# One TensorE stream, another order: the weighted sum between scores 1 and 2, misc work behind score 3

## The chip, the cores and the metric

The kernel runs on one core of a Trainium2 chip. Its time is the device time of one execution in microseconds (us), the median of three runs. TensorE (PE) multiplies matrices, VectorE (DVE) and ScalarE (ACT) work on rows of elements, GpSimd (POOL) does small work and indirect transfers, SyncE (SP) issues most transfers. The engines run their own instruction streams and wait for each other on semaphores.

## The reference, cut to what matters

```
x: (8, 512, 128); 16 heads of 8; 8 experts of 256, top 2
h = layernorm(x) * (1 + ca) + sa
q, k, v = h @ binarized(Wq, Wk, Wv).T + biases        # per head: 512 x 8
att = softmax(q k^T / sqrt(8)); y = att v; x = x + ga * (y @ Wp' + bp)
h = layernorm(x) * (1 + cb) + sb
x = x + gb * (shared_expert(h) + sum over the top 2 experts of weight * expert(h))
```

The attention is computed for 8 batches x 16 heads x 512 queries x 512 keys. That is where the change lies. The experts follow it.

## The kernel before, in words

**Batches and slots.** The attention of a batch is cut into 16 slots (SLOTS). Slot n holds four heads of group n // 4 and 128 keys (n % 4). For each of the four heads hh it makes a score tile of 128 keys x 512 queries (`scores`, `st`), which ScalarE exponentiates into `pt` (`exponentials`), and a weighted sum of all four heads (`products`, `pv`) which adds into one PSUM bank over eight slots. The sum of slot n-1 is issued in slot n. After eight slots ScalarE copies the bank to `y_strips` (`evacuate_y`), and the first sum of the next eight waits for that copy (`y_evacuated`).

**Maxima.** A softmax needs each query's maximum over all keys before its scores are used. Eight slots ahead of their use, TensorE computes the same scores in the other orientation (`max_scores`, a pair of matmuls into one of two `mx` banks, half heads each), and VectorE reduces a pair to the negative maximum (`maxima`, `neg_max`). A slot holds two such pairs, called A and B here; slots 0 to 4 of the first batch hold three. `max_T` turns the maxima of four heads into rows, `split_max` on VectorE splits them, and SyncE stores them as extra rows of the queries' stack, so that a score comes out with its maximum already taken off.

**Banks.** Scores alternate between two banks, so score hh waits until the exponential two before it is done. Maxima alternate between two banks as well, so a pair waits until VectorE has reduced the pair two before it. In the last eight slots of the last batch there are no maxima left; scores 2 and 3 then use the free `mx` banks, and a score waits for the exponential four before it (`wide`).

**Misc work.** Everything else shares a single bank, `misc`: projections and transposes of the batch two ahead, of the one before, router logits, ranks. The use of this bank is a fixed chain: each user waits until the evacuation of the one before it is done (`free(done)` on `misc_free`). `between` issues what belongs to a slot: m1, m2, m3 (`max_T`) in slots 1, 5, 9, y1, yT, out in 2, 3, 4, ln1 in 7, q in 8, h2T in 10, y0 in 11, lg (`router_logits`) in 12, k in 14. Behind the weighted sum stand v (`project_v`) in slot 0, m0 for the next batch in 12 and ranks in 15. VectorE and ScalarE take up the results of misc in the same slot: ScalarE behind its four exponentials, VectorE at the place that the change moves. Their larger pieces are `residual_sum` and `stats2` (slot 4), `split_max` and `layer_norm1` (5), `layer_norm2` (7), `likeliest` (13), `choose` (14), `assign_rows` (15).

**Order.** The order is written out by hand in the `body` functions. On TensorE a slot is: score 0, score 1, pair A, misc, score 2, pair B, score 3, weighted sum of slot n-1.

Of the kernel before, what the change touches and what calls it, by code (L numbers as in the profile page):

```python
# [18 lines left out]
SLOTS = G * TT  # L19
# [28 lines left out]
def adaln_block(nc: bass.Bass, x, Wq, bq, Wk, bk, Wv, bv, Wp, bp, sh_gate, sh_up, sh_down,  # L48
                gate_w, up_w, down_w, router_w, routing_bias, c, wmod, out):
    ctx = ExitStack()  # L50
    with ctx:
# [904 lines left out]
        def _(dve):  # L956
# [163 lines left out]
            def body(b, first, last):  # L1120
                for n in range(SLOTS):
                    fills = fills_at(b, n)
                    maxima(fills[0])
                    if n == 0 and first:
                        for i, w in enumerate("qk"):
                            first_part(dve, B1, i, use(AHEAD, w + "_1"))
# [22 lines left out]
                        add_router_bias(b.plus(-1), use(b, "lg"))  # L1149
                    if n in (13, 14) and not first:  # L1150
                        (likeliest, choose)[n - 13](b.plus(-1))
                    maxima(fills[1])
                    if n == 12 and not last:
                        split_max(b.plus(1), 0, use(b, "m0"))
                    if n == 15 and not first:
# [164 lines left out]
        def _(pe):  # L1320
# [203 lines left out]
            def between(b, n, first, last):  # L1524
# [25 lines left out]
                if n == 14 and b.const < B - 2:  # L1550
                    project(1, use(b, "k"))

            def body(b, first, last):
                for n in range(SLOTS):
                    g, j = n // TT, n % TT
                    fills = fills_at(b, n)
                    if j == 0:
                        pe.wait_ge(m_row_loaded[g % 2], ROW_DMAS * (2 * b.n + g // 2 + 1))
                        if b.const == 0 and g < DIRECT:
                            pe.wait_ge(stack_loaded[0][g], STACK_DMAS)  # L1560
                    scores(b, n, 0)
                    scores(b, n, 1)
                    for f in fills[0]:
                        max_scores(*fill_of(f))
                    between(b, n, first, last)
                    scores(b, n, 2)
                    for f in fills[1][:1]:
                        max_scores(*fill_of(f))
                    scores(b, n, 3)
                    for f in fills[1][1:]:  # L1570
                        max_scores(*fill_of(f))

                    if n > 0:
                        products(b, n - 1)
                    elif not first:
                        products(b.plus(-1), SLOTS - 1)
                    if n == 0 and not last:
                        project_v(use(b, "v"))
                    if n == 12 and not last:
                        max_T(b.plus(1), 0, use(b, "m0"))  # L1580
                    if n == 15 and not first:
                        ranks(b.plus(-1), use(b, "rank"))
# [132 lines left out]
```

## Time and profile before

| | us |
|---|---|
| median of 3 runs | 664.68 |
| lowest, highest | 662.48, 667.34 |
| the profiled execution's span | 683.7 |
| attention in it, first to last exponential | 41.9 to 482.3 |
| a steady batch in it | 55.8 |

The page gives each engine's busy share: TensorE 91%, VectorE 76%, ScalarE 60%, GpSimd 39%. The profiled execution is longer than the plain runs; its rows are used for durations and for the order of things. In a timeline, instructions of one form that follow each other are one row: its start, the time from the first start to the last end, and their count. The end of a matmul is modelled, so the distance of two starts is the better measure of what a matmul costs.

### The profile page before, as it was taken

What the parts mean: (1) busy time and instruction counts of PE and PEld (TensorE: products, weight loads), DVE (VectorE), ACT (ScalarE), POOL (GpSimd) and SP (SyncE); (2) the same over time, 40 slices, a digit from 0 to 9 for tenths busy, and PEclk for the clock granted to TensorE, in tenths of its full rate; (3) what the DMA queues carried; (4) which work ended last, traced back from release to release, by engine and by line L of the source; (5) the groups of instructions that cost most, each with busy time, mean ns of one, the idle gap of its engine ahead of it and who ended that gap; (6) DMA issues with size and microseconds to landing.
All of it is one profiled execution on the core that took longest, in us unless ns stands there. A gap on an engine that the chain in (4) does not pass through costs nothing.

```text
span 683.7 us, 11593 instructions
## 1 busy us (share of the span) xinstructions
PE 624.5 (91%) x3693; PEld 298.9 (44%) x3693; DVE 516.7 (76%) x1104; ACT 411.0 (60%) x846; POOL 264.0 (39%) x309
## 2 busy tenths in 40 slices
PE   4988999999999999999999999999998898888935
PEld 2332333233333333433333333232465888888931
DVE  5659888889988989888898888983368655555617
ACT  2145777777777687777777777778542445444520
POOL 4221022324352461452434233134434366566540
PEclk9669999999999999999999999999999999999987
DMA  3533132222321233223222231115102222222228
GB/s 101 146 56 97 52 101 76 66 82 72 94 86 62 75 97 95 79 78 105 72 70 75 70 98 52 39 40 173 53 0 70 64 74 78 69 78 79 70 68 320
DMA packets 50064, 56.92 MB, mean 83 GB/s; under 512 B 10281, under 2 KB 39243, under 8 KB 50004
## 3 DMA queue, kind: packets, MB, share of 16 engines
q1 hardware_dynamic: 42648, 43.11, 22.4%
q0 software_dynamic: 4320, 8.47, 3.6%
q10 hardware_dynamic: 3036, 4.61, 2.1%
q8 instruction: 30, 0.49, 0.3%
q14 instruction: 30, 0.25, 0.1%
HBM read 38.36 MB, written 17.92 MB: 82 GB/s over the span
## 4 chain that ended last, share of the span: by engine, by line
PE 68%; DVE 13%; ACT 6%; DMA 4%; issue 4%; SPq 2%; POOL 1%; another core or an unknown queue 0%; ACTq 0%; POOLq 0%; DVEq 0%
PE pv L1457 15%; PE st L1446 14%; PE mx L1431 13%; PE st L1646 9%; DVE neg_max L1012 6%; PE mx L1590 3%; ACT pt L803 2%; PE misc L1324 2%; PE misc L1351 2%; PE pv L1655 2%; PE misc L1655 2%; PE st L1600 1%; PE misc L1357 1%; DMA even_qk<-k_parts 1%; DVE ln L969 1%
## 5 line engine op out<-in xcount | busy, mean ns | idle before, releaser
L803 ACT ACTIVATE pt<-st 128x512 f32<-128x512 f32 x496 | 282.2, 598 | 106.0 <-PE st L1446 96.8
L1012 DVE TENSOR_REDUCE neg_max<-mx 128x2 f32<-128x1024 f32 x248 | 294.4, 1215 | 50.5 <-PE mx L1431 47.3
L1457 PE MATMUL pv<-pt,vs 128*32 128x512 f32 x1024 | 136.4, 605 | 0.3 <-ACT pt L803 0.3
L690 POOL DMA_INDIRECT routed<-rec,row_u x64 | 64.4, 1007 | 142.1 <-PE pv L1457 115.2
L750 POOL DMA_INDIRECT results<-qs,home_u x71 | 77.4, 1091 | 60.5 <-ACT qs L932 42.1
L1446 PE MATMUL st<-even_qk 74*128 74x512 bf16 x256 | 88.9, 388 | 4.1 <-DMA even_qk<-m_rows 2.2
L1446 PE MATMUL st<-qs,ks 74*128 74x512 bf16 x240 | 81.5, 383 | 1.8 <-ACT pt L803 1.1
L1431 PE MATMUL mx<-even_qk 72*128 72x512 bf16 x240 | 74.5, 392 | 6.0 <-DVE neg_max L1012 3.4
L1431 PE MATMUL mx<-ks,qs 72*128 72x512 bf16 x256 | 76.5, 380 | 2.8 <-DVE neg_max L1012 2.5
L1258 DVE TENSOR_TENSOR vs<-vs,st 128x256 f32<-128x256 f32 x71 | 29.7, 418 | 42.6 <-ACT vs L927 31.4
L1646 PE MATMUL st<-vs,pt 128*128 128x128 f32 x376 | 52.0, 282 | 10.3 <-DVE vs L1258 7.4
L398 POOL TENSOR_TENSOR qk_r<-qk_f,qk_parts 128x512 f32<-128x512 f32 x15 | 17.4, 1163 | 108.6 <-DVE qk_parts L390 108.4
L927 ACT ACTIVATE vs<-st 128x256 f32<-128x256 f32 x71 | 27.4, 386 | 45.7 <-PE st L1646 35.1
L1446 PEld LDWEIGHTS st<-even_qk 74*128 74x128 bf16 x256 | 20.7, 98 | 73.2 <-ACT pt L803 51.6
L1646 PEld LDWEIGHTS st<-vs,pt 128*128 128x128 f32 x376 | 46.8, 196 | 12.8 <-ACT vs L922 9.1
L1446 PEld LDWEIGHTS st<-qs,ks 74*128 74x128 bf16 x240 | 18.9, 98 | 67.5 <-ACT pt L803 51.6
L1457 PEld LDWEIGHTS pv<-pt,vs 128*32 128x32 f32 x1024 | 20.1, 108 | 52.9 <-issue 38.1
L1431 PEld LDWEIGHTS mx<-even_qk 72*128 72x128 bf16 x240 | 22.3, 100 | 37.9 <-DVE neg_max L1012 11.6
L1431 PEld LDWEIGHTS mx<-ks,qs 72*128 72x128 bf16 x256 | 23.8, 98 | 31.0 <-DVE neg_max L1012 7.8
L1270 DVE COPY pt<-even_qk 128x768 f32 x47 | 27.6, 588 | 6.2 <-issue 3.1
L1590 PE MATMUL mx<-h2T,shared_w 128*128 128x512 f32 x64 | 29.9, 600 | 1.9 <-issue 1.9
L1646 PE MATMUL st<-vs 128*128 128x128 f32 x192 | 25.9, 278 | 3.7 <-DVE vs L1258 2.5
(199 smaller groups left out, 792.7 us busy)
## 6 DMA issues: line engine op xcount, KB each, us to landing
ks<-routed SPq DMA_DIRECT2D x71, 65.0 KB
even_qk<-q_parts SPq DMA_DIRECT2D x48, 96.0 KB
qs<-q_parts SPq DMA_DIRECT2D x48, 96.0 KB
ks<-k_parts SPq DMA_DIRECT2D x48, 96.0 KB
even_qk<-k_parts SPq DMA_DIRECT2D x42, 96.0 KB
q_parts<-qk_parts SPq DMA_DIRECT2D x21, 128.0 KB
k_parts<-qk_parts SPq DMA_DIRECT2D x7, 384.0 KB, 2.3
x_in<-L_attn_x SPq DMA_DIRECT2D x8, 256.0 KB
```

The costliest lines, as they stand in the source:

```text
L690: pool.indirect_dma_start(out=routed_dram, out_offset=bass.IndirectOffsetOnAxis(ap=row_u[:, k, t:t + 1], axis=0), in_=rec[b.par][:, k, t, ...
L750: pool.indirect_dma_start(out=result_dram, out_offset=bass.IndirectOffsetOnAxis(ap=home_u[:, slot:slot + 1], axis=0), in_=y_u[slot], in_of ...
L803: act.activation(pt[n % 2][:, hh, :], score_bank(b, n, hh), ACT.Exp, scale=SCALE).then_inc(exp_done, 1)
L927: act.activation(silu_u[slot % 2], st_bank[slot % 2][:, 0:I], ACT.Silu).then_inc(silu_ready, 1)
L1012: dve.tensor_reduce(neg_max[g % 2][:, hh, 2 * half:2 * half + 2], mx_bank[half][:], AX_X, ALU.max, negate=True).then_inc(mx_free, 1)
L1258: dve.tensor_tensor(act_u[slot % ARING], silu_u[slot % 2], st_bank[slot % 2][:, I:2 * I], ALU.mult).then_inc(act_ready, 1)
L1270: dve.tensor_copy(w_unit[u % WRING], weights.rearrange("p e i -> p (e i)")[:, bass.ds(first, 3 * I)]).then_inc(w_ready, 1)
L1431: last = pe.matmul(mx_bank[half][:, t, :], qs[b.par][0:PROD, h, q0:q0 + P], ks[b.par][0:PROD, h, :], start=True, stop=True)
L1446: pe.matmul(score_bank(b, n, hh), ks[b.par][0:STACK, h, j * P:(j + 1) * P], qs[b.par][0:STACK, h, :], start=True, stop=True).then_inc(st_f ...
L1457: last = pe.matmul(pv_bank[32 * hh:32 * (hh + 1), :], vs[b.par][:, j, HG * g + hh, :], pt[n % 2][:, hh, :], start=(n % Y_SLOTS == 0), stop ...
L1590: last = pe.matmul(mx_bank[j][:, which, :], shared_w[:, IC * which + j, :], h2T[:, T * b:T * (b + 1)], start=True, stop=True)
L1646: last = pe.matmul(st_bank[slot % 2][:, m * P:(m + 1) * P], w_unit[u % WRING][:, m * P:(m + 1) * P], xuT[slot % 2], start=True, stop=True)
```

## The change

On TensorE a slot is now: score 0, pair A, score 1, weighted sum of slot n-1, score 2, pair B, score 3, misc. The work that stood behind the sum (v, m0, ranks) stays last. On VectorE both reductions of a slot stand ahead of the slot's misc work, which stood between them. ScalarE's, GpSimd's and SyncE's programs are the same. No instruction is added or taken away.

```
--- before.py
+++ after.py
@@ -1121,6 +1121,7 @@
                 for n in range(SLOTS):
                     fills = fills_at(b, n)
                     maxima(fills[0])
+                    maxima(fills[1])
                     if n == 0 and first:
                         for i, w in enumerate("qk"):
                             first_part(dve, B1, i, use(AHEAD, w + "_1"))
@@ -1149,7 +1150,6 @@
                         add_router_bias(b.plus(-1), use(b, "lg"))
                     if n in (13, 14) and not first:
                         (likeliest, choose)[n - 13](b.plus(-1))
-                    maxima(fills[1])
                     if n == 12 and not last:
                         split_max(b.plus(1), 0, use(b, "m0"))
                     if n == 15 and not first:
@@ -1550,6 +1550,13 @@
                 if n == 14 and b.const < B - 2:
                     project(1, use(b, "k"))
 
+            def weigh(b, n, first):
+
+                if n > 0:
+                    products(b, n - 1)
+                elif not first:
+                    products(b.plus(-1), SLOTS - 1)
+
             def body(b, first, last):
                 for n in range(SLOTS):
                     g, j = n // TT, n % TT
@@ -1559,21 +1566,17 @@
                         if b.const == 0 and g < DIRECT:
                             pe.wait_ge(stack_loaded[0][g], STACK_DMAS)
                     scores(b, n, 0)
-                    scores(b, n, 1)
                     for f in fills[0]:
                         max_scores(*fill_of(f))
-                    between(b, n, first, last)
+                    scores(b, n, 1)
+                    weigh(b, n, first)
                     scores(b, n, 2)
                     for f in fills[1][:1]:
                         max_scores(*fill_of(f))
                     scores(b, n, 3)
                     for f in fills[1][1:]:
                         max_scores(*fill_of(f))
-
-                    if n > 0:
-                        products(b, n - 1)
-                    elif not first:
-                        products(b.plus(-1), SLOTS - 1)
+                    between(b, n, first, last)
                     if n == 0 and not last:
                         project_v(use(b, "v"))
                     if n == 12 and not last:
```

TensorE, slots 11 and 12 of a steady batch (`st` a score, `mx` a pair of maxima, `pv` the sum, `y_strips` the transposes of y0, `router_T` the logits, `neg_max` max_T). Before:

```order
L1457 MATMUL pv<-pt,vs 32x512 x4
L1446 MATMUL st<-qs,ks 128x512 x2
L1431 MATMUL mx<-even_qk 128x512 x2
L1393 MATMUL misc<-router_T,h2T_now 128x8 x4
L1446 MATMUL st<-qs,ks 128x512
L1431 MATMUL mx<-even_qk 128x512 x2
L1446 MATMUL st<-qs,ks 128x512
L1457 MATMUL pv<-pt,vs 32x512 x4
L1364 MATMUL misc<-ident,neg_max 16x128
```

With the change:

```order
L1446 MATMUL st<-qs,ks 128x512
L1431 MATMUL mx<-even_qk 128x512 x2
L1446 MATMUL st<-qs,ks 128x512
L1457 MATMUL pv<-pt,vs 32x512 x4
L1446 MATMUL st<-qs,ks 128x512
L1431 MATMUL mx<-even_qk 128x512 x2
L1446 MATMUL st<-qs,ks 128x512
L1393 MATMUL misc<-router_T,h2T_now 128x8 x4
L1364 MATMUL misc<-ident,neg_max 16x128
```

The logits stood between scores 1 and 2 and max_T behind the sum; now they follow each other directly.

TensorE, slots 13 and 14 of the last batch, where scores 2 and 3 go to `mx`. Before:

```order
L1457 MATMUL pv<-pt,vs 32x512 x4
L1446 MATMUL st<-qs,ks 128x512 x2
L1446 MATMUL mx<-qs,ks 128x512 x2
L1457 MATMUL pv<-pt,vs 32x512 x4
L1446 MATMUL st<-qs,ks 128x512 x2
L1446 MATMUL mx<-qs,ks 128x512 x2
L1457 MATMUL pv<-pt,vs 32x512 x4
```

With the change:

```order
L1446 MATMUL st<-qs,ks 128x512 x2
L1457 MATMUL pv<-pt,vs 32x512 x4
L1446 MATMUL mx<-qs,ks 128x512 x2
L1446 MATMUL st<-qs,ks 128x512 x2
L1457 MATMUL pv<-pt,vs 32x512 x4
L1446 MATMUL mx<-qs,ks 128x512 x2
L1446 MATMUL st<-qs,ks 128x512 x2
```

All four scores of a slot stood ahead of the sum; now the sum splits them into two and two.

VectorE, slots 12 and 13 of a steady batch (`neg_max` a reduction, `m_rows` the split of m0, `probs` the begin of `likeliest`). Before:

```order
L1012 TENSOR_REDUCE neg_max<-mx 128x2 x2
L1045 TENSOR_TENSOR logits<-misc,router_bias 128x32
L1012 TENSOR_REDUCE neg_max<-mx 128x2
L1020 CAST m_rows<-misc 16x128
L1022 TENSOR_TENSOR m_rows<-misc,m_rows 16x128
L1012 TENSOR_REDUCE neg_max<-mx 128x2
L1057 TENSOR_SCALAR probs<-probs 128x32
```

With the change:

```order
L1012 TENSOR_REDUCE neg_max<-mx 128x2 x2
L1045 TENSOR_TENSOR logits<-misc,router_bias 128x32
L1020 CAST m_rows<-misc 16x128
L1022 TENSOR_TENSOR m_rows<-misc,m_rows 16x128
L1012 TENSOR_REDUCE neg_max<-mx 128x2 x2
L1057 TENSOR_SCALAR probs<-probs 128x32
```

Rows of one form that follow each other are one, across slots too. Before, the first row holds B of slot 11 and A of slot 12, and A of slot 13 stands alone ahead of `probs`; now it holds both of slot 12, and both of slot 13 stand ahead of `probs`. In slots 4 and 5 the order of the rows reads the same, but they are A4, misc, B4, A5, misc, B5, A6 before and A4, B4, misc, A5, B5, misc, A6 now.

## Rows read from the trace of the kernel before

**Rows 1.** Cores view, whole run.

```profile
core 0: 683.7 us, clock 0.971
```

**Rows 2.** Page, part 1: busy us (share) xinstructions.

```profile
PE 624.5 (91%) x3693; PEld 298.9 (44%) x3693; DVE 516.7 (76%) x1104; ACT 411.0 (60%) x846; POOL 264.0 (39%) x309
```

**Rows 3.** Windows: us, busy of PE, PEld, DVE, ACT, POOL, granted clock, DMA, GB/s.

```profile
277.30:333.10 55.80, 54.56 (x317) 19.42 (x321) 49.59 (x100) 41.37 (x75) 22.92 (x26) 1.00 0.28 80
465.40:482.30 16.90, 16.25 (x110) 5.22 (x106) 4.32 (x29) 15.81 (x33) 6.15 (x8) 1.00 0.65 192
```

**Rows 4.** Waits in batch 4: waiting, releaser: us in total, times, longest.

```profile
PEld st L1446 <- ACT pt L803: 12.9, 23, 0.8
```

**Rows 5.** Timeline, slot 6: start us, us, engine line op out<-in xcount [idle before].

```profile
291.86 0.60 PE L1446 MATMUL st<-even_qk 74*128 74x512 bf16 x2
...
292.29 1.68 ACT L803 ACTIVATE pt<-st 128x512 f32<-128x512 f32 x3 [0.72 <-PE st L1446]
292.30 0.60 PE L1431 MATMUL mx<-even_qk 72*128 72x512 bf16 x2
...
292.94 0.39 PE L1446 MATMUL st<-even_qk 74*128 74x512 bf16 x1
...
293.95 0.60 PE L1431 MATMUL mx<-even_qk 72*128 72x512 bf16 x2 [0.62 <-DVE neg_max L1012]
...
294.39 0.38 PE L1446 MATMUL st<-even_qk 74*128 74x512 bf16 x1
...
294.70 1.06 PE L1457 MATMUL pv<-pt,vs 128*32 128x512 f32 x8
...
295.70 0.60 PE L1446 MATMUL st<-even_qk 74*128 74x512 bf16 x2
...
296.77 1.22 DVE L1012 TENSOR_REDUCE neg_max<-mx 128x2 f32<-128x1024 f32 x1 [0.62 <-PE mx L1431]
```

**Rows 6.** Timeline, slot 1 of batch 5, TensorE.

```profile
331.04 0.60 PE L1431 MATMUL mx<-ks,qs 72*128 72x512 bf16 x2
...
332.02 0.39 PE L1446 MATMUL st<-qs,ks 74*128 74x512 bf16 x1 [0.19 <-ACT pt L803]
```

**Rows 7.** Windows: slots 4 to 6 of batch 4 as VectorE sees them.

```profile
285.94:296.78 10.84, 10.13 (x59) 3.42 (x58) 10.15 (x22) 6.83 (x13) 4.31 (x6) 1.00 0.21 65
```

**Rows 8.** Timeline, VectorE, slots 4 and 5.

```profile
287.08 0.68 DVE L1039 TENSOR_TENSOR x<-misc,x_ep 128x512 f32<-128x512 f32 x1
...
288.86 2.32 DVE L1012 TENSOR_REDUCE neg_max<-mx 128x2 f32<-128x1024 f32 x2
291.10 0.27 DVE L1020 CAST m_rows<-misc 16x128 bf16<-16x128 f32 x1
...
292.69 3.47 DVE L1012 TENSOR_REDUCE neg_max<-mx 128x2 f32<-128x1024 f32 x3
```

**Rows 9.** Timeline, slot 12 of batch 4, TensorE.

```profile
313.39 0.95 PE L1393 MATMUL misc<-router_T,h2T_now 128*128 128x8 f32 x8
314.20 0.38 PE L1446 MATMUL st<-even_qk 74*128 74x512 bf16 x1
```

**Rows 10.** Timeline, slot 8 of batch 4: projection of q, its evacuation, y_strips.

```profile
299.85 1.02 PE L1351 MATMUL misc<-hT,wT 128*128 128x512 f32 x2
...
302.27 0.68 ACT L788 ACTIVATE qk_f<-misc,bias_qkv 128x512 f32<-128x512 f32 x1
302.85 0.60 ACT L809 ACTIVATE y_strips<-pv 128x512 f32<-128x512 f32 x1
```

**Rows 11.** Timeline, batch 7: slots 7, 8, 14 and 15.

```profile
459.38 0.60 PE L1446 MATMUL st<-qs,ks 74*128 74x512 bf16 x2
...
464.32 1.09 ACT L803 ACTIVATE pt<-mx 128x512 f32<-128x512 f32 x2 [0.38 <-PE mx L1446]
...
479.27 1.09 ACT L803 ACTIVATE pt<-mx 128x512 f32<-128x512 f32 x2
...
481.23 1.09 ACT L803 ACTIVATE pt<-mx 128x512 f32<-128x512 f32 x2
```

More of the change, by code:

```diff
@@ L1123, in body @@
                     maxima(fills[0])
+                    maxima(fills[1])
                     if n == 0 and first:
@@ L1151, in body @@
                         (likeliest, choose)[n - 13](b.plus(-1))
-                    maxima(fills[1])
                     if n == 12 and not last:
@@ L1551, in between, with weigh @@
                     project(1, use(b, "k"))
+            def weigh(b, n, first):
+                if n > 0:
+                    products(b, n - 1)
+                elif not first:
+                    products(b.plus(-1), SLOTS - 1)
             def body(b, first, last):
@@ L1561, in body @@
                     scores(b, n, 0)
-                    scores(b, n, 1)
                     for f in fills[0]:
                         max_scores(*fill_of(f))
-                    between(b, n, first, last)
+                    scores(b, n, 1)
+                    weigh(b, n, first)
                     scores(b, n, 2)
@@ L1571, in body @@
                         max_scores(*fill_of(f))
[L1573 to L1576, printed above, removed]
+                    between(b, n, first, last)
                     if n == 0 and not last:
```

## The prediction

> **What bounds the kernel now.** I read the page first, then one batch at a time, then the waits, and at last single rows of three slots. TensorE is busy for 91% of the span [rows 2], and in a steady batch for 54.56 of 55.80 us, at full clock [rows 3]. So only a wait of TensorE is worth anything. The busy figure hides short waits, since the ends of matmuls are modelled; starts show them. In slot 6 of batch 4 [rows 5] matmuls of 512 columns follow each other every 0.22 us (two scores from 291.86, maxima pair from 292.30), the last score leads to the weighted sum after 0.31 (294.39 to 294.70), and that to the next score after 1.00. A slot without misc work is thus 0.44 + 0.44 + 0.22 + 0.44 + 0.31 + 1.00 = 2.85 us. This one has two waits more. Score 2 starts at 292.94 and could at 292.74: 0.20 for the exponential of score 0 (the two score banks alternate). Pair B starts at 293.95 and could at 293.16: 0.79 for VectorE. From all starts of this batch, read likewise, I count 3.2 us of waits in 55.80: 0.20 for ScalarE in each of slots 6, 13, 15 and 0; 0.2 and 0.8 for VectorE in slots 5 and 6; 0.2 and 0.2 in 14 and 15; 0.43 in slot 1, where max_T waits for the evacuation of v and score 2 behind it (pair A at 331.04, 0.44 for it and 0.11 for max_T make 331.59, and score 2 starts at 332.02) [rows 6]; 0.33 in slot 9; 0.1 in slots 2 and 5. [Rows 4] give ScalarE 12.9 us, but as idle time of the weight loads, most of which lies under a running sum; only the starts of matmuls count. These 3.2 us are all that the change can win: 3.2 x 6.5 = 21 us at most.
>
> Three latencies carry the rest [rows 5]. Score start to its exponential: 0.43 (291.86 to 292.29). Exponential start to the score that reuses its bank: 0.65 (292.29 to 292.94). So a score may start 1.08 after the one two before it. Start of a maxima pair to its reduction: 0.63 (295.70 + 0.44 to 296.77). Reductions on VectorE follow each other every 1.13, and TensorE goes on 0.06 after an end.
>
> **The change, part by part.** The profiled execution took 683.7 us of span [rows 1], more than the 664.68 median of the plain runs; the stages are not known for the latter, so I work in microseconds of difference and add them to the median.
>
> *Scores.* New order: s0, pair A, s1, sum, s2, pair B, s3, misc. From s0 to s2 are now 0.22 + 0.44 + 0.31 + 1.00 = 1.97, far over 1.08: the old wait goes. But from s2 to the next s0 are 0.22 + 0.44 + 0.22 = 0.88 plus misc, and 1.08 are needed: the same 0.20 comes back there, in slots whose misc work is under 0.20. Formerly misc filled s0 to s2, now it fills s2 to s0. Plain slots: 3.05 before and after. It only matters where misc that stood behind the sum now fills the gap: v in slot 0 (-0.2) and ranks in slot 15 (-0.1).
>
> *Misc behind score 3.* In slot 1 max_T comes 2 us later, so v has been evacuated: 0.43 becomes 0.10, -0.3. Slot 9 likewise on the side of ScalarE: -0.2. Against these stand two new waits. **Slot 12**: router logits and max_T for the next batch now stand back to back on one bank. VectorE must add the bias between. Logits take 0.81 of TensorE (313.39 to 314.20) [rows 9], so max_T could start 1.03 after s3. VectorE reaches the bias when reduction B is done: it starts at -0.44 + 0.63 = 0.19, hands over at 1.32, the bias takes 0.2, and TensorE goes at 1.58: +0.55. **Slot 9**: the sum of slot 8 starts a new accumulation and waits for y_strips. ScalarE does evac q first. The projection (299.85, 1.02 us) starts 0.22 after s3, so its result is there at 1.3; y_strips follows 0.58 later and lasts 0.60 (302.27, 302.85) [rows 10], done at 2.5. The sum, now early in slot 9, could start at 0.22 + 0.86 + 0.22 + 0.44 + 0.31 = 2.05: +0.45. Before, it stood 2 us later and waited for nothing.
>
> *VectorE.* Pair A comes 0.22 sooner, pair B 0.9 later, and misc stands behind both. The tight stretch is slots 4 to 6, where VectorE has run through: from 285.94 to 296.78, 10.15 of 10.84 us busy [rows 7], 1.78 of misc in slot 4 (287.08 to 288.86) and 1.59 in slot 5 (291.10 to 292.69) [rows 8]. After the change its unbroken run begins with B of slot 4, 0.19 after s3. Its queue is B4, misc, A5, B5, misc, A6: 0.19 + 1.13 + 1.78 + 1.13 + 1.13 + 1.59 + 1.20, so A of slot 6 ends at 8.15. Pair A of slot 7 starts at 8.21 and can be reduced at 8.84. A of slot 4 could be reduced 1.78 before s3 (pair A is 2.41 before s3). The three slots take 10.62, before 10.84: -0.2. The wait hardly shrinks, since the same work runs without a pause; it only moves from pair B to pair A. In slots 13 to 15 the same reckoning gives one wait of 0.2 for two: -0.2. In slot 1 the split and stats (1.57) now delay A of slot 2: +0.2.
>
> A steady batch: -0.2 -0.1 -0.3 -0.2 +0.55 +0.45 -0.2 -0.2 +0.2 = 0.0. Batches 1 to 5: 0. Ends, for what I could not see (whether the two new waits are met in full, or hidden by a VectorE that lags; whether the lag of slots 13 to 2 adds up): -0.6 to +0.9 a batch, the lower end with both new waits half hidden, the upper end with the 0.79 of [rows 5] met once more. Batch 6 has no projections and a lighter VectorE; its heaviest wait (0.8) shrinks: -0.4. Batch 0, with three pairs in slots 0 to 4, is bound by VectorE already; max_T of slot 2 comes later and its row is wanted in slot 4: 0 to +1, I take +0.5.
>
> *The last eight slots.* Here there are no maxima, and scores 2 and 3 have banks of their own, so all four scores of a slot run ahead while ScalarE works off the last. It goes without a pause: pairs of exponentials at 479.27 and 481.23, 1.96 a slot [rows 11]. The sum of n-1 needs the fourth exponential of n-1. It now stands ahead of scores 2 and 3. Let that exponential end at 0: sum at 0.06, s2 at 1.06, its exponential at 1.49. ScalarE has only two in stock, 0.99 us: it idles 0.5. The fourth starts at 1.98, ends at 2.57. So 2.57 a slot, not 1.96: +0.6 in slots 10, 14, 15. Slots 11 to 13 have other ScalarE or misc work and took 2.5 to 3.0 before: -0.3 together. Slot 9, where the sum waits for y_strips: 3.06 for 2.69, +0.4. Entry: from s0 of slot 7 (459.38) to the end of slot 8's exponentials (464.32 + 1.09) were 6.03 [rows 11]; now s3 is at 2.63, s1 of slot 8 at 3.71, sum 4.02, s2 5.02, end at 5.02 + 0.43 + 1.09 = 6.54: +0.5. Sum 3 x 0.6 - 0.3 + 0.4 + 0.5 = **+2.4 us**. What follows hangs on the end of this stage and shifts by it. Ends: 0 (if some slots hide it) to 8 x 0.6 = +5.
>
> Sum: 0 - 0.4 + 0.5 + 2.4 = +2.5, less 0.2 for waits in the first half of batch 7, where VectorE has less to do: +2.3. **664.7 + 2.3 = 667.0 us.**
>
> **Rivals.** (1) My forecast, no measurable change, within 1% (6.6 us; about what this measurement can tell from none): 0.62.
>
> (2) Faster: VectorE's slack. A bank's pair returns every 3.05 us and needs 0.63 + 1.20 + 0.06, so a reduction may be 1.2 us late before TensorE waits; formerly B stood close behind A and had 1.0; if the lag of slots 4 to 6 and 13 to 15 fits in, their 1.4 us of waits go, and if max_T and the sum of slot 9 hide too, a batch wins 1.6: 6.5 x 1.6 = 10, less 2.4: 657 us. For it: the waits are short. Against it: [rows 7] leave VectorE 0.7 us in three slots. 0.17.
>
> (3) Slower: VectorE stands idle before B with misc behind it. A ends 1.78 - 1.20 = 0.58 us before s3, B can start 0.19 after it: up to 0.77 a slot in which the old order ran misc. It decides where a slot with misc follows another before the lag has been worked off (misc over 0.7 in each: 1 and 2, 4 and 5, 13 to 15). If 0.77 is lost once in each of two such groups, +1.5 a batch, 6.5 x 1.5 + 2.4 = +12: 677 us. Against it: a VectorE that lags does not idle, and my walk of slots 4 to 6 shows no pause. 0.19. The Trainium skill, page TensorE: Matmul & The Clock Gate, section Architectural detail, says that VectorE's queue is strict first in, first out; by that rule no misc operation can pass the waiting reduction. The trace agrees so far: at 296.77 VectorE had idled 0.62 before a reduction, and nothing ran there [rows 5].
>
> (4) The last slots leave TensorE idle 0.6 in 2.57, and the granted clock falls there to the lower level (1.2 GHz). The clock was 1.00 in every stage of [rows 3], the last eight slots with waits too. At half clock the sum alone takes 1.0 us more in each of seven slots, +7: 676 us, 0.02. The same page, section A second HAM failure mode, tells of a clock that swings when TensorE idles briefly again and again; no run here shows it.
>
> **The numbers.** Range: cases (1) and (2), (3) in part: 659 to 673 us. The lower end is 6 x -0.6 = -3.6 and no cost in the last slots, with 2 us for a part of (2); the upper is 6 x 0.5 plus 5. Faster by over 1%: 0.16. Within: 0.62. Slower: 0.22.
>
> **What would show it.** Steady batches of 55.8 +- 0.6; plain slots still 3.05, with the wait before s0, not s2; max_T of slot 12 some 0.5 late behind the bias; the first sum of slot 9 late behind y_strips; slots 4 to 6 still with one wait for VectorE of 0.8, before pair A; slots 14 and 15 of batch 7 at 2.57. Batches under 55 refute the VectorE walk, over 56.5 mean rival (3); last slots at 1.96 refute the largest term.

## The result, and the profile after

| | us |
|---|---|
| before, median (4 runs) | 664.66 |
| changed, median (4 runs; 674.1 to 684.79) | 678.91 |
| ratio, without the slowest run (median of the other three: 676.65) | 1.0195 [1.0141, 1.0249] |
| the same kernel measured again on another chip (6 runs; before 666.09 there) | 673.63, ratio 1.0135 [1.0097, 1.0173] |

The change makes the kernel slower by 1.4 to 2%. 667.0 was predicted. The run of 684.79 us fell in a slower state of the chip, with a lower clock, and the ratio leaves it out. The changed kernel's profiled execution took 674.1 us; cores view and page, part 1:

```profile
core 0: 672.4 us, clock 0.964
...
PE 619.8 (92%) x3693; PEld 299.4 (45%) x3693; DVE 524.6 (78%) x1104; ACT 418.5 (62%) x846; POOL 263.8 (39%) x309
```

They answer to [rows 1] and [rows 2]. The two profiled spans must not be compared: that of before (683.7) has a slow expert stage behind the attention, 201.4 us from the last exponential to the end, against 180.7 here and 180.5 in a kernel of the experiments that takes as long as before (e3). VectorE's total can be compared: 524.6 us, 7.9 more than before for the same 1104 instructions. Windows of the changed kernel (us, busy of PE, PEld, DVE, ACT, POOL, granted clock, DMA, GB/s), batch 4 and batch 2, each from the weighted sum of slot 1 to the next, then the last batch from its first exponential to its last:

```profile
281.20:337.80 56.60, 54.29 (x314) 19.61 (x313) 51.07 (x101) 41.72 (x75) 22.62 (x27) 1.00 0.26 79
166.20:224.60 58.40, 55.93 (x314) 19.88 (x313) 51.30 (x101) 41.72 (x75) 22.81 (x27) 0.97 0.26 77
443.52:491.74 48.22, 43.71 (x263) 14.48 (x263) 29.69 (x74) 37.60 (x71) 15.40 (x18) 1.00 0.28 84
```

The last batch of the kernel before, cut the same way:

```profile
436.92:482.33 45.41, 43.58 (x263) 13.93 (x261) 28.11 (x69) 37.27 (x70) 15.45 (x18) 1.00 0.29 90
```

Batch 4 takes 56.60 against 55.80 [rows 3], with VectorE busy for 51.07 against 49.59. Batch 2 takes 58.4, at a clock of 0.97. The last batch takes 2.8 more. It is cut at exponentials because the sum has moved inside its slot. The attention's last exponential ends at 491.7 against 482.3, and what follows it is as long as in e3, so the loss lies ahead of it. Its first exponential starts at 45.1 against 43.8 (the table of times before has 41.9 for it), and over all executions this start varies from 42.7 to 47.7. From first to last the attention takes 446.7 against 438.6.

**The wait that was not in the prediction.** Timeline of the changed kernel, TensorE, slots 15 to 1 (start us, us, engine line op out<-in xcount [idle before]):

```profile
335.18 1.05 PE L1357 MATMUL misc<-wT,hT 128*128 128x128 f32 x8
336.07 0.38 PE L1446 MATMUL st<-qs,ks 74*128 74x512 bf16 x1
337.10 0.61 PE L1431 MATMUL mx<-ks,qs 72*128 72x512 bf16 x2 [0.65 <-DVE neg_max L1012]
```

Pair A of slot 1 could start 0.22 after score 0, at 336.29, and starts at 337.10: 0.81 lost, behind slot 15 of each of batches 1 to 5. The same stretch on VectorE:

```profile
333.46 0.41 DVE L390 CAST qk_parts<-qk_f 128x512 bf16<-128x512 f32 x1
333.80 0.18 DVE L1082 TENSOR_TENSOR place<-misc,next_row 128x32 f32<-128x32 f32 x1
333.90 0.15 DVE L1084 TENSOR_TENSOR next_row<-next_row,misc 128x8 f32<-128x8 f32 x1
334.01 1.18 DVE L1086 TENSOR_TENSOR picked<-chosen,place 128x64 f32<-128x64 f32 x1
335.23 0.22 DVE L1089 TENSOR_REDUCE row_f<-picked 128x8 f32<-128x64 f32 x1
335.48 0.43 DVE L1092 CAST row_u<-row_f 128x8 uint32<-128x8 f32 x1
335.83 3.47 DVE L1012 TENSOR_REDUCE neg_max<-mx 128x2 f32<-128x1024 f32 x3
```

and on GpSimd:

```profile
333.96 1.15 POOL L398 TENSOR_TENSOR qk_r<-qk_f,qk_parts 128x512 f32<-128x512 f32 x1 [16.98 <-DVE qk_parts L390]
```

The cast at 333.46 (`first_part` of k) lets GpSimd go at 333.96, and for these 1.15 us VectorE's product `picked` stands: 1.18 us for 128 x 64 elements. All products of a run, changed kernel (duration ns, least, median, most):

```profile
L1086 DVE TENSOR_TENSOR picked<-chosen,place x8: 224/1178/1182, 162.3 to 521.1; 128x64 f32<-128x64 f32 x8
```

and the kernel before:

```profile
L1086 DVE TENSOR_TENSOR picked<-chosen,place x8: 224/225/226, 160.0 to 511.7; 128x64 f32<-128x64 f32 x8
```

Before, reduction B stood between cast and product, 1.14 us, and GpSimd was through. With both maxima moved ahead of the misc work, the two are neighbours. The Trainium skill, page GPSIMD Engine Reference, section Specifications, says that GpSimd shares its SBUF interfaces with VectorE, with contention for VectorE instructions that have two SBUF inputs. The product has two; the trace agrees, with 0.22 against 1.18 us.

**The waits that were.** Changed kernel, TensorE, behind the logits of slot 12:

```profile
320.82 0.95 PE L1393 MATMUL misc<-router_T,h2T_now 128*128 128x8 f32 x8
322.18 0.28 PE L1364 MATMUL misc<-ident,neg_max 128*16 128x128 f32 x1 [0.41 <-DVE logits L1045]
```

The logits take 0.81 [rows 9], max_T could start at 321.63 and starts at 322.18: 0.55. The first sum of slot 9 and the pair of slot 7:

```profile
308.35 0.38 PE L1446 MATMUL st<-even_qk 74*128 74x512 bf16 x1
309.22 0.64 PE L1457 MATMUL pv<-pt,vs 128*32 128x512 f32 x4 [0.49 <-ACT y_strips L809]
```

```profile
299.52 0.81 PE L1446 MATMUL st<-even_qk 74*128 74x512 bf16 x2
300.93 0.61 PE L1431 MATMUL mx<-even_qk 72*128 72x512 bf16 x2 [0.61 <-DVE neg_max L1012]
```

309.22 could be 308.66: 0.56. The row of 299.52 holds score 3 of slot 6 and score 0 of slot 7, 0.41 apart; the pair could start 0.22 behind the latter, at 300.15: 0.78 lost, in place of the 0.79 before pair B [rows 5]. In the last slots ScalarE's exponentials read (changed kernel):

```profile
488.10 1.08 ACT L803 ACTIVATE pt<-mx 128x512 f32<-128x512 f32 x2 [0.50 <-PE mx L1446]
...
490.66 1.08 ACT L803 ACTIVATE pt<-mx 128x512 f32<-128x512 f32 x2 [0.50 <-PE mx L1446]
```

Before, such pairs stood without a gap, 1.96 a slot [rows 11]; now ScalarE idles 0.50 in each, and sums follow each other every 2.56.

### The profile page after: what moved, and what is told of

Read it like the earlier page. It is cut to its first block, busy times and chain, and to the rows that moved or that the text cites. A ratio compares the mean times of both kernels' runs of the same rounds, so it can differ in the third digit from the quotient of the medians.

```text
span 672.4 us, 11593 instructions
## 1 busy us (share of the span) xinstructions
PE 619.8 (92%) x3693; PEld 299.4 (45%) x3693; DVE 524.6 (78%) x1104; ACT 418.5 (62%) x846; POOL 263.8 (39%) x309
## 4 chain that ended last, share of the span: by engine, by line
PE 61%; DVE 25%; DMA 4%; ACT 4%; issue 3%; POOL 1%; SPq 1%; ACTq 0%; POOLq 0%; DVEq 0%
PE pv L1457 14%; DVE neg_max L1012 13%; PE mx L1431 12%; PE st L1446 11%; PE st L1649 8%; PE mx L1593 3%; PE misc L1658 2%; PE pv L1658 2%; PE misc L1324 2%; PE misc L1351 2%; ACT pt L803 2%; DVE stats_sb L961 1%; PE st L1603 1%; DMA even_qk<-k_parts 1%; PE mx L1638 1%
## 5 line engine op out<-in xcount | busy, mean ns | idle before, releaser
L803 ACT ACTIVATE pt<-st 128x512 f32<-128x512 f32 x496 | 286.6, 599 | 106.9 <-PE st L1446 97.4
L1446 PE MATMUL st<-even_qk 74*128 74x512 bf16 x256 | 99.3, 390 | 2.1 <-DMA even_qk<-m_rows 1.6
L1446 PE MATMUL st<-qs,ks 74*128 74x512 bf16 x240 | 90.8, 383 | 0.8 <-ACT pt L803 0.2
L1446 PEld LDWEIGHTS st<-even_qk 74*128 74x128 bf16 x256 | 24.9, 97 | 88.9 <-ACT pt L803 68.5
L1446 PEld LDWEIGHTS st<-qs,ks 74*128 74x128 bf16 x240 | 23.1, 97 | 75.6 <-ACT pt L803 61.8
L1649 PE MATMUL st<-vs,pt 128*128 128x128 f32 x376 | 49.7, 275 | 0.0
L1593 PE MATMUL mx<-h2T,shared_w 128*128 128x512 f32 x64 | 31.4, 628 | 1.9 <-DVE pt L1162 1.9
L901 ACT ACTIVATE pt<-mx 128x512 f32<-128x512 f32 x16 | 9.6, 597 | 29.4 <-PE mx L1593 29.3
```

The source lines that it names most:

```text
L803: act.activation(pt[n % 2][:, hh, :], score_bank(b, n, hh), ACT.Exp, scale=SCALE).then_inc(exp_done, 1)
L1446: pe.matmul(score_bank(b, n, hh), ks[b.par][0:STACK, h, j * P:(j + 1) * P], qs[b.par][0:STACK, h, :], start=True, stop=True).then_inc(st_f ...
L1593: last = pe.matmul(mx_bank[j][:, which, :], shared_w[:, IC * which + j, :], h2T[:, T * b:T * (b + 1)], start=True, stop=True)
L1649: last = pe.matmul(st_bank[slot % 2][:, m * P:(m + 1) * P], w_unit[u % WRING][:, m * P:(m + 1) * P], xuT[slot % 2], start=True, stop=True)
```

## The experiments

The kernels ran in four groups of four, each group on one chip with runs of the kernel before beside them (664.24, 683.4, 664.66 and 666.09 us; the second chip has a slower expert stage). Ratios are to these; durations from traces are of the attention alone, where a steady batch repeats to 0.1 us in the kernel before and to 0.5 us in the variants. A label as e3 names a run.

**The collision in slot 15.** Row assignment ahead of the first part of k:

```
-                    if n == 15 and b.const < B - 2:
-                        first_part(dve, b.plus(2), 1, use(b, "k"))
 ...
                         assign_rows(b.plus(-1), use(b, "rank"))
+                    if n == 15 and b.const < B - 2:
+                        first_part(dve, b.plus(2), 1, use(b, "k"))
```

> The changed kernel, but in slot 15 VectorE does assign_rows ahead of the first part of k, whose result starts a 1.15 us operation on GpSimd. Collision theory: the product in assign_rows takes 0.23 us again instead of 1.18, the cast behind it 0.26 instead of 0.43, the wait of 0.8 us before pair A of slot 1 is gone, a steady batch takes 55.8 us instead of 56.6, the attention ends 4 to 5 us earlier than in the changed kernel (490.2). Lag theory (VectorE is simply later because misc stands behind both reductions): the product may be short, but the order of two pieces of one slot changes no lag; the wait of 0.8 us and the batch of 56.6 us stay.

Measured: ratio 1.0098 [1.006, 1.0136]. The products and a batch:

```profile
L1086 DVE TENSOR_TENSOR picked<-chosen,place x8: 224/225/226, 163.2 to 518.1; 128x64 f32<-128x64 f32 x8
```

```profile
166.60:222.30 55.70, 54.03 (x316) 19.73 (x315) 49.76 (x101) 41.58 (x76) 22.81 (x27) 1.00 0.27 80
```

0.9 less than 56.60, by two statements that change places. Without the collision the batch is where the prediction had it (55.8). Then the collision was put into the kernel before, by taking reduction B of slot 15 ahead of the first part of k:

```
+                    if n == 15:
+                        maxima(fills[1])
                     if n == 15 and b.const < B - 2:
                         first_part(dve, b.plus(2), 1, use(b, "k"))
```

> The kernel before, with one reduction moved: in slot 15 reduction B stands ahead of the first part of k, so that assign_rows follows that part directly. Collision theory: the product in assign_rows takes 1.18 us here too, and some 0.3 to 0.9 us a batch come on top (2 to 5 us in all). Lag theory: product 0.23 us, time within 1 us of the kernel before.

Measured: ratio 1.0013 [0.9989, 1.0037].

```profile
L1086 DVE TENSOR_TENSOR picked<-chosen,place x8: 224/1178/1180, 159.8 to 511.6; 128x64 f32<-128x64 f32 x8
```

```profile
277.00:332.80 55.80, 54.57 (x318) 19.42 (x320) 50.73 (x101) 41.37 (x76) 22.86 (x26) 1.00 0.28 80
```

The collision is there, VectorE is busy for 1.1 us more (50.73), and the batch costs nothing. The cost that was expected did not come. So it costs only where VectorE has no time to spare, as in the new order in slots 15 to 1; e9 below, with the old order on TensorE, has the collision too and also loses nothing.

**The last slots.** In slots without maxima (`wide`) the sum goes back behind score 3:

```
-                    weigh(b, n, first)
+                    if not wide(b, n):
+                        weigh(b, n, first)
 ...
+                    if wide(b, n):
+                        weigh(b, n, first)
```

> The changed kernel, but in the last eight slots of the last batch the weighted sum stands behind score 3 again. If the split into two and two costs ScalarE its stock there, slots 14 and 15 go back from 2.56 to 1.97 us and the attention ends 2.2 us earlier than in the changed kernel; nothing else moves. If that stage is bound by something else, they stay at 2.56.

Measured: ratio 1.0171 [1.0145, 1.0196]; the last batch:

```profile
443.03:487.84 44.81, 43.85 (x263) 14.34 (x263) 29.29 (x72) 37.07 (x71) 15.43 (x18) 1.00 0.31 90
```

44.8 against 48.2 (before: 45.4): 3.4 back, one us more than the term of +2.4. The profiled execution is the fastest of the five (669.98), though it had two stretches at half clock (below). The other four took 673 to 677 us, so the plain runs show little of the gain, and no trace of them tells why.

**The logits.** They were moved ahead of the sum, so that their bias would be done before max_T:

```
                     scores(b, n, 1)
+                    if n == 12 and not first:
+                        router_logits(use(b, "lg"))
                     weigh(b, n, first)
```

> The changed kernel, but the router logits stand behind score 1, ahead of the weighted sum; max_T for the next batch stays at the end of slot 12. If the bank hand-over logits, bias, max_T is what lengthens slot 12 (4.31 us from sum to sum against 3.64), it takes 3.7 now and a batch 56.0 instead of 56.6 (six batches, -3.5 us). If VectorE's lag is what it waits for, the gain is under 0.2 a batch.

Measured: ratio 1.0349 [1.032, 1.0378]. TensorE in slot 12:

```profile
263.75 0.38 PE L1446 MATMUL st<-qs,ks 74*128 74x512 bf16 x1
264.71 1.06 PE L1393 MATMUL misc<-router_T,h2T_now 128*128 128x8 f32 x8 [0.58 <-DVE y_tok L1031]
...
268.93 0.28 PE L1364 MATMUL misc<-ident,neg_max 128*16 128x128 f32 x1 [1.20 <-DVE logits L1045]
```

The expectation failed twice. The logits now wait for the bank of y0, which VectorE still has to divide; and max_T starts as late behind the last score as in the changed kernel (1.57 us, 1.58 there), because the bias stands behind reduction B, whatever time the logits are ready. As no logits fill that time now, TensorE waits there for 1.36 us instead of 0.55, and a batch without a stretch at half clock takes 57.7. What delays max_T is VectorE's queue, not the logits.

**max_T one slot later.** In the changed kernel max_T for the next batch and its split go to slot 13:

```
-                   ["lg", "m0"], [], ["k"], ["rank"]]
+                   ["lg"], ["m0"], ["k"], ["rank"]]
 ...
-                    if n == 12 and not last:
+                    if n == 13 and not last:
                         split_max(b.plus(1), 0, use(b, "m0"))
```

> The changed kernel, but max_T for the next batch and its split stand in slot 13, no longer behind the logits in slot 12. The wait of 0.55 us for the bias goes, and in slot 13 max_T covers 0.1 us of the wait for ScalarE: a steady batch 56.0 instead of 56.6, six batches 3.5 to 4 us. On the clock: if the waits of slot 12 are what lets the granted clock fall for one stretch in batches 2 and 3 (at 208 in the changed kernel, 206 and 264 in the two variants), no such stretch is left in the attention, and the mean clock rises to that of the kernel before (0.97). If the stretches come by chance or from another wait (slot 9), they stay.

Measured: ratio 1.0177 [1.0133, 1.0222]; batch 56.4, and a new wait in slot 14:

```profile
226.90:283.30 56.40, 54.29 (x314) 19.54 (x313) 50.71 (x101) 41.52 (x75) 22.73 (x27) 1.00 0.31 89
```

```profile
273.56 1.12 PE L1351 MATMUL misc<-hT,wT 128*128 128x512 f32 x2 [0.24 <-DVE m_rows L1022]
```

The wait of slot 12 is gone, and 0.40 is back before the projection of k, whose bank VectorE hands over only with the split behind `likeliest`: score 3 starts at 272.94, the projection could at 273.16. The batch won 0.2 where 0.6 was expected. The move also costs once: slot 13 of batch 0 takes 4.9 us instead of 3.1. In e8, e12 and e16, which put a further user of the bank there too, it is longer as well (5.2 to 5.9). No stretch at half clock fell into batches 0 to 7.

**y_strips.** ScalarE copies them ahead of its evacuation of q in slot 8:

```
+                    if n == Y_SLOTS:
+                        evacuate_y(b, 0)
                     if n == 8 and b.const < B - 2:
                         evacuate_qk(b.plus(2), 0, use(b, "q"))
```

> The changed kernel, but in slot 8 ScalarE copies y_strips ahead of the evacuation of q. Then the copy is done 1.5 us after score 3 instead of 2.5, the first sum of slot 9 finds it done, and its wait of 0.56 us goes: slot 9 3.7 us instead of 4.23, batches 0 to 5, -3.3 us. If the wait were for the fourth exponential or the weights, slot 9 stays at 4.23. Clock stretches in the attention: as before the edit if slot 12 makes them, gone if slot 9 does.

Measured: ratio 1.009 [1.0039, 1.0142].

```profile
220.90:277.00 56.10, 54.27 (x318) 19.56 (x318) 51.14 (x101) 41.60 (x75) 22.67 (x27) 1.00 0.31 90
```

A batch wins the 0.5 that [rows 10] had led to.

**The wait of slot 12 in the old order.** In the kernel before, the bias goes behind reduction B and max_T ahead of the sum, so that TensorE waits there too:

```
                     maxima(fills[1])
+                    if n == 12 and not first:
+                        add_router_bias(b.plus(-1), use(b, "lg"))
 ...
+                    if n == 12 and not last:
+                        max_T(b.plus(1), 0, use(b, "m0"))
```

> The kernel before, with the hand-over of slot 12 made bad: VectorE adds the router bias behind reduction B, and max_T for the next batch stands ahead of the weighted sum. TensorE then waits there until 1.58 us after score 3, 1.3 us longer, in batches 1 to 6: +8 us. On the clock: if such a wait is what makes the granted clock fall, this kernel shows stretches at half clock near slots 12 and 13, which the kernel before never does, and comes out up to 2 us slower for each; if they belong to the new order of the sum, it shows none.

Measured: ratio 1.0347 [1.0309, 1.0386]. The wait, and windows behind it (the second in batch 2):

```profile
271.82 0.38 PE L1364 MATMUL misc<-ident,neg_max 128*16 128x128 f32 x1 [1.20 <-DVE logits L1045]
```

```profile
271.80:275.20 3.40, 3.38 (x12) 0.72 (x13) 0.56 (x2) 0.78 (x3) 0.00 (x0) 0.50 0.18 58
210.40:220.50 10.10, 9.96 (x30) 2.60 (x31) 5.01 (x20) 3.59 (x7) 0.00 (x0) 0.50 0.22 62
```

In five of six batches TensorE's granted clock falls to half (1.2 GHz) within this wait, which lasts 1.3 us; such a batch takes 58.7 to 61.3 us instead of 55.8. The kernel before has no such stretch from 50 to 633 us. So the new order as such isn't needed for it. A wait in a stretch that is dense otherwise goes ahead of it or holds its start.

**All repairs at once.** The four that were tried alone (row assignment first, old last slots, max_T one slot later, y_strips first) together:

> The changed kernel with all four repairs: assign_rows ahead of the first part of k, y_strips first on ScalarE, max_T for the next batch in slot 13, old order in the last eight slots. If the four terms add (0.8, 0.55 and 0.6 us a batch, 2.2 at the end), a steady batch takes 54.6 us, the attention 436 us long against 445.1 changed and 438.6 before, and the kernel 659 to 662 us, the first faster than before. If VectorE's lag takes over when TensorE waits less, the batches stay above 55.2 and the kernel at 664.

Measured: ratio 0.9999 [0.9961, 1.0038]. Batch 3, and the two stretches at half clock of this execution:

```profile
225.70:281.10 55.40, 54.23 (x314) 19.50 (x313) 50.19 (x101) 41.32 (x77) 22.71 (x27) 1.00 0.32 91
...
100.70:107.40 6.70, 6.70 (x20) 2.08 (x20) 2.45 (x2) 2.77 (x5) 0.00 (x0) 0.50 0.47 134
438.60:445.20 6.60, 6.60 (x29) 1.38 (x21) 4.97 (x13) 2.59 (x5) 0.00 (x0) 0.50 0.30 89
```

0.4 less than before in a batch. Batches 1 to 5 win 2.8 us together; batches 0, 6 and 7, with the two stretches and the long slot 13 of batch 0, lose 6.3.

**Each half of the change alone.** VectorE's half in the kernel before, both reductions ahead of the misc work:

```
                     maxima(fills[0])
+                    maxima(fills[1])
 ...
-                    maxima(fills[1])
                     if n == 12 and not last:
```

> The kernel before with the change's VectorE half alone: both reductions of a slot ahead of its misc work, TensorE's order as before. Theory (the loss comes from TensorE's new order, which makes VectorE the late engine in slots 15 to 1, 4 to 6 and 12): here pair B follows pair A within 1.1 us, so VectorE does not idle between them, and the misc work only comes 1.13 later; one new wait of 0.2 in slot 12 (max_T behind the bias behind reduction B). The product in slot 15 takes 1.18 again, at no cost, since TensorE is not waiting there. Batch 55.8 to 56.3, ratio 1.000 to 1.006. Rival (the loss comes from reductions ahead of misc, whatever TensorE does): batch 56.6, ratio 1.01 to 1.02.

Measured: ratio 1.0009 [0.9976, 1.0042], batch 55.8.

```profile
281.00:336.80 55.80, 54.44 (x317) 19.23 (x319) 51.26 (x101) 41.45 (x75) 22.96 (x26) 1.00 0.29 80
```

TensorE's half alone (the changed kernel with the statement put back):

> The changed kernel with VectorE's old order: reduction A, misc work, reduction B. TensorE issues misc behind score 3, that is after pair B, so VectorE waits for misc with B's pair already there. Theory: B is reduced 1 to 2 us later than its pair allows in slots 1, 4, 5, 11, 12, 13 and 15, TensorE waits before the pairs of the slots that follow, and the two halves of the change need each other: batch 58 to 62, ratio 1.03 to 1.08, with stretches at half clock behind the longest waits. Rival (VectorE's order matters little, as the slack of 1.2 us of a bank covers it): batch 56 to 57, ratio 1.01 to 1.02 as in the changed kernel.

Measured: ratio 1.0357 [1.0295, 1.0419], batch 57.5, with three waits before pairs (0.7, 1.1 and 0.7 us), such as

```profile
304.78 0.60 PE L1431 MATMUL mx<-even_qk 72*128 72x512 bf16 x2 [0.96 <-DVE neg_max L1012]
```

for which a reduction was late. The batch came out 0.5 under the range expected. So the loss comes with TensorE's order: VectorE's half costs nothing alone, and repairs a part of what TensorE's half does.

**A version that is faster than both?** Three repairs (slot 15, y_strips, last slots) with max_T left where it was:

> The changed kernel with the three repairs that paid alone: row assignment ahead of the first part of k in slot 15 (-0.8 a batch), y_strips ahead of the evacuation of q in slot 8 (-0.55), and the weighted sum behind score 3 in the last eight slots (-2.9 once). max_T for the next batch stays directly behind the logits in slot 12. Theory of added terms: batch 56.6 - 0.8 - 0.55 = 55.2 to 55.4, ratio 0.992 to 0.998 if no stretch at half clock falls into the attention, +0.3% for each that does. Rival (the late engine is VectorE, and a repair only moves its wait): batch 55.7, ratio 1.000 to 1.005.

Measured: ratio 0.9987 [0.9951, 1.0022], batch 55.2 as the theory had it, but the ratio lies above the theory's 0.992 to 0.998. Its profiled execution had two stretches at half clock in batches 1 to 6, and half clock up to 78 us. The same with the misc work of slots 11 to 13 evened out:

```
-        ... ["y0"], ["lg", "m0"], [], ["k"], ["rank"]]
+        ... ["lg"], ["m0"], ["y0"], ["k"], ["rank"]]
```

> The same three repairs, and the misc work of slots 11 to 13 spread so that no slot holds two users of the bank: logits with their bias and exponential in slot 11, max_T for the next batch with its split and the begin of the choice of experts in slot 12, transposes and division of y0 in slot 13. Theory: max_T of slot 12 no longer waits (-0.55), and VectorE's misc work of slots 13 and 14 is lighter: batch 54.6 to 55.0, ratio 0.985 to 0.993; with no wait over 0.3 us in slots 12 and 13, TensorE's clock falls there less often. Rival (the waits return elsewhere, as when max_T alone was moved to slot 13: -0.65 in one slot, +0.5 in another): batch 55.2 to 55.4, ratio 0.995 to 1.000.

Measured: ratio 0.9971 [0.9932, 1.001].

```profile
221.70:277.10 55.40, 53.96 (x318) 19.65 (x318) 50.05 (x101) 41.36 (x77) 22.75 (x27) 1.00 0.31 91
```

```profile
321.28 0.61 PE L1431 MATMUL mx<-ks,qs 72*128 72x512 bf16 x2 [0.72 <-DVE neg_max L1012]
```

The rival held: max_T waits no more, and pair A of slot 14 waits instead (score 0 at 320.18, so 0.88 lost): it needs the reduction of pair A of slot 13, which VectorE begins only after split and `likeliest`. With `likeliest` back in slot 13:

> The kernel with misc spread over slots 11 to 13, but the begin of the choice of experts back in slot 13, ahead of the division of y0: slot 12 then has only max_T and its split. With both in slot 12, the slot took 4.17 and 3.70 followed in 13. Theory: VectorE is late either way, and only the place of the wait changes: slot 12 to 13 now 3.5, slots 13 and 14 together 0.5 longer, batch 55.3 to 55.5, ratio 0.994 to 1.000. Rival: the work is even now and the wait goes, batch 54.9 or less, ratio 0.988 to 0.993.

Measured: ratio 0.9988 [0.9962, 1.0013], batch 55.1; the wait is 0.52 now and one slot later. Neither is measurably faster than before. In their traces the attention takes 435.8 and 435.6 us against 438.6, a gain of 0.4% that the plain runs can't tell from none.

**The changed kernel twice more**, with nothing edited:

> The changed kernel itself, once more, beside kernels of the same chip. Its profiled execution was 6.5 us longer in the attention than that of before, but the plain runs differ by 13. Theory (the rest is half clock that falls into the attention by chance of the execution): the profile again shows batches of 56.6 where no stretch at half clock lies, the plain runs scatter over 10 us with their clock, ratio 1.012 to 1.020, attention 444 to 452 us. Rival (the profiled execution hides something that costs 1 us more in every batch): ratio 1.018 to 1.025 with fastest runs over 1.015 as well.

> The changed kernel a third time, for one more trace: slots 12 to 14 show either 4.31 / 3.05 / 3.70 (full clock) or 4.3 / 4.6 to 5.3 / 3.7 to 4.6 (a stretch at half clock). Theory: between none and three stretches in the attention after the first batch, nearly all just behind the 1.3 us wait of slot 12. Rival (they come anywhere): most lie in other slots.

Measured: 673.63 (ratio 1.0135 [1.0097, 1.0173]) and 673.08. A batch of the one profile and of the other:

```profile
222.00:280.10 58.10, 55.80 (x318) 20.00 (x317) 50.72 (x101) 41.72 (x75) 22.74 (x27) 0.97 0.31 87
```

```profile
280.70:337.20 56.50, 54.19 (x314) 19.64 (x313) 50.87 (x101) 41.74 (x75) 22.67 (x27) 1.00 0.27 79
```

The first has four such batches (2 to 5), the second none: from first to last exponential 450.7 and 444.9 us. The place is the same each time, the slot behind the wait for the bias (first profile, TensorE and a window):

```profile
262.92 0.28 PE L1364 MATMUL misc<-ident,neg_max 128*16 128x128 f32 x1 [0.40 <-DVE logits L1045]
...
264.00 1.91 PE L1457 MATMUL pv<-pt,vs 128*32 128x512 f32 x8
```

```profile
264.10:267.50 3.40, 3.40 (x12) 0.62 (x13) 1.17 (x2) 1.19 (x2) 0.00 (x0) 0.50 0.15 39
```

The sum takes 1.91 us instead of 1.07. A stretch costs 1.5 us: a batch with one takes 58.0 against 56.5 between first exponentials, and (450.7 - 444.9) / 4 gives the same. The execution without a stretch took 673.08 us, 1.0% more than before there; the one with four took 675.84, though its attention began 3.5 us earlier. The rival, a cost that the first profile did not show, finds no support: batches without a stretch repeat at 56.5 to 56.9.

**One piece alone, in the old order.** max_T of slots 1 and 9 behind score 3, its split behind reduction B:

```
+                    if n in (1, 9) and not first:
+                        max_T(b, n // 4 + 1, use(b, f"m{n // 4 + 1}"))
```

> The kernel before with one piece of the change: max_T of slots 1 and 9 behind score 3, and its split behind reduction B. TensorE then no longer waits there for ScalarE's evacuation: by the trace of before, 0.33 in slot 1 and 0.23 to 0.33 in slot 9 go. Theory: batch 55.8 - 0.5 = 55.3, ratio 0.993 to 0.998. Rival (the split behind B makes VectorE late for pair A of slots 2 and 10, as in every repair here one wait turns into another): batch 55.7 to 56.0, ratio 0.999 to 1.004.

Measured: ratio 1.014 [1.0105, 1.0175], batch 57.3: the expectation failed, and by more than its rival.

```profile
282.20:339.50 57.30, 54.75 (x314) 19.27 (x313) 50.17 (x101) 41.31 (x76) 22.86 (x26) 1.00 0.27 78
```

```profile
284.67 0.66 PE L1326 MATMUL misc<-ident,y_strips 128*128 128x128 f32 x4 [0.48 <-DVE m_rows L1022]
```

The next user of the bank stands in the front half of slot 2 in this order, and waits 0.64 for the split; in slot 10 it is 0.70. Neither wait for ScalarE in slots 1 and 9 goes, and they grow by 0.2 and 0.1, since max_T no longer fills the time before score 2. Together that makes up the 1.5 us of the batch. Work behind score 3 pays only if the misc work of the slot after it is late too.

## Why the prediction was wrong

**The step that failed** is the last of the part on VectorE: "In slots 13 to 15 the same reckoning gives one wait of 0.2 for two: -0.2", and so the "= 0.0" of a steady batch. The reckoning took VectorE's durations from before. One of them, the product of slot 15, is 0.225 only because a reduction stood between it and the cast that releases GpSimd. In the new order it is 1.18, and the cast behind it 0.43 instead of 0.26, so that the row assignment takes 2.03 us (333.80 to 335.83) and pair A of slot 1 waits 0.81. Five batches: +4. e1 takes it away and gives a batch of 55.7. In the sum, the term is -0.2 forecast and +0.6 measured (0.17 before A of slot 0, and 0.81 before A of slot 1, for 0.4 before). The prediction gave this term no reason why the durations would stay, and none of its rivals named it.

**The clock.** Rival (4) gave 0.02 to a fall of the granted clock in the last eight slots. They run at 1.00. It falls in slots 13 and 14 instead, behind the very wait that the prediction had priced at 0.55: 1, 4 and 0 times in three profiled executions, 1.5 us each. The step "Slot 12: +0.55" had the wait right and left out what can follow from it. e7 shows the link in the old order; what decides whether the clock falls in a given passage stays open. Of rival (3), the price (677 us) was near by luck: VectorE does not idle more, it is busier (in batch 4 it idles 5.5 us against 6.2 before).

**Right**: plain slots 3.05; slot 12 +0.55 (0.55); slot 9 +0.45 (0.56); slots 4 to 6 one wait of 0.8 before pair A (0.78); the mechanism of the last slots (2.56 a slot for 2.57). **Off in size**: the last batch, +2.4 less 0.2 forecast, +2.8 measured, and by e2 the new order of its last eight slots costs 3.4. Slots 11 to 13 gave nothing back where -0.3 was forecast, and the entry cost 0.7 instead of 0.5. Batch 6, -0.4 forecast, took 0.2 more than before: its slot 12 has the new wait too. Batch 0, +0.5 forecast, took 0.1 more. **The range**: its upper end was added up from 0.5 a batch, though the part on VectorE had ended at +0.9; by the latter it would be 675, still under the 678.91 measured first.

**The sum, corrected.** The attention from first to last exponential, the kernel before and the changed kernel's execution without a stretch at half clock:

```profile
43.77:482.33 438.56, 426.75 (x2423) 147.60 (x2421) 373.00 (x720) 324.21 (x590) 152.49 (x175) 0.99 0.27 79
...
46.20:491.09 444.89, 424.18 (x2423) 150.13 (x2421) 380.50 (x723) 326.95 (x590) 151.52 (x175) 0.99 0.27 78
```

That is +6.3 us where +2.3 was forecast: 0.1 in batch 0, 3.4 in batches 1 to 6 and 2.8 in the last. The 4.0 us between are the size of the collision's five waits; the other misses nearly cancel. 664.7 + 6.3 = 671.0, inside the range of the forecast. One to four stretches add 1.5 to 6: 672.5 to 677. The 676.65 of the first measurement lies at the upper end of this, the 673.63 of the second within it; no trace of its two slowest runs exists, so why they took 681 and 685 us stays open.

## What to carry to other kernels

A duration in a profile holds for its neighbours: before an operation is moved, look up what other engines the operation ahead of it releases, and whether they then run beside it. Price a new wait of TensorE inside a dense stretch not only at its length: ask whether the granted clock falls behind it. And where two engines are both busy for nine tenths of a stage and more, here 55 and 50 of 55.8 us, a wait that is removed can come back in a later slot (e5, e12); those of e1 and e6 did not. Seven kernels with repairs brought the batch to between 55.1 and 56.4 us, and none was measurably faster than the kernel before.

## What the runs showed of the hardware

- A VectorE product of 128 x 64 elements from two SBUF tiles takes 0.225 us alone and 1.18 beside GpSimd's product of 128 x 512 (1.15 us). Its median in a trace is 1.18 in the seven kernels where the cast that releases GpSimd stands directly ahead, and 0.22 in the nine others. Of the reductions from PSUM that run beside the same GpSimd work in the kernel before, none is longer (1.22).
- The granted clock falls to one half for one stretch, 3.4 us in the changed kernel, up to 6.8 in its variants, 10 us in e7, in some executions and not in others. In eight profiled executions with the wait of slot 12 in the new order (0.55 us, 1.36 in e4) it did so 13 times in the 48 passages of batches 1 to 6, each time beginning 0.9 to 1.4 us after max_T started behind that wait. In e7 it did so in five of six, beginning within the wait. In the nine executions of kernels with no wait or a shorter one there (before among them) it did so three times in 54, and one of these, in e10, began 1.2 us after a max_T that had waited for 0.43.
